# Y products three chunks ahead and a reordered opening in a fused graph-attention and linear kernel

## The reference

```python
def gnn(input1, input2, adj, a1, a2):
    e = input1 @ a1 + (input2 @ a2).T
    e = jnp.where(e > 0, e, 0.2 * e)
    att = jnp.where(adj > 0, e, -9e15)
    att = jax.nn.softmax(att, axis=1)
    att = att * jnp.sum(adj, axis=1, keepdims=True)
    att = 0.1 * att + 0.9 * adj
    return att @ input2
x = x + gnn(layernorm(x), input2, adj, a1, a2)
x = x + layernorm(x) @ weight.T + bias
```

## Time and profile before

| | us |
|---|---|
| median of 3 runs | 385.27 (384.86 to 386.11) |
| profiled execution | 384.49 |
| its span, first to last instruction | 382.7 |

### The profile page before, as it was taken

One profiled execution on the slowest core, in us unless ns is written; L12 is line 12 of the kernel. 1 busy time (PEld: TensorE's weight loads), 2 busy tenths in 40 slices (PEclk: granted clock), 3 DMA queues, 4 the chain that ended last, 5 costly groups with the idle time before them and its releaser, 6 DMA issues.

```text
span 382.7 us, 8770 instructions
## 1 busy us (share of the span) xinstructions
PE 360.1 (94%) x3195; PEld 313.7 (82%) x3195; DVE 311.0 (81%) x791; ACT 246.9 (65%) x630; POOL 136.3 (36%) x257
## 2 busy tenths in 40 slices
PE   1589999999999999999999999999999999999991
PEld 1477888888888888888888888888888888888880
DVE  5999889989978787796968778698887979889633
ACT  4798989787661947658192856839294776777010
POOL 4598041515250706144160705326070613110111
PEclk9999999999999999999999999999999999999997
DMA  7999996666668989799998988996867610010000
GB/s 254 231 214 213 223 184 143 122 141 122 143 16 163 111 125 146 63 210 18 196 77 151 120 82 188 20 221 50 184 89 118 151 29 15 0 16 16 14 15 16
DMA packets 21769, 44.12 MB, mean 115 GB/s; under 512 B 5078, under 2 KB 13020, under 8 KB 21724
## 3 DMA queue, kind: packets, MB, share of 16 engines
q0 software_dynamic: 9216, 33.56, 61.1%
q1 hardware_dynamic: 12508, 9.98, 9.4%
HBM read 74.97 MB, written 2.11 MB: 201 GB/s over the span
## 4 chain that ended last, share of the span: by engine, by line
PE 85%; DVE 6%; ACT 5%; issue 1%; DMA 1%; SPq 0%; POOLq 0%; POOL 0%; DVEq 0%
PE acc_y L660 23%; PE acc_v L660 22%; PE acc_u L660 22%; PE acc_u L651 6%; PE acc_v L651 6%; PE acc_y L651 4%; ACT steep L488 3%; PE small L645 2%; DVE plus L998 2%; DMA plus<-in 1%; PE turned L620 1%; ACT minus L545 1%; ACT weights_v L536 1%; ACT weights_u L530 0%; DVE plus L875 0%
## 5 line engine op out<-in xcount | busy, mean ns | idle before, releaser
L488 ACT ACTIVATE steep<-s_bc,steep_s 128x256 bf16<-128x256 f32 x512 | 209.2, 497 | 80.8 <-DMA s_bc<-s_rows 74.8
L660 PE MATMUL acc_y<-weights_y,adj_all 128*128 128x257 f16 x896 | 103.7, 275 | 2.0 <-DVE lin L896 1.3
L875 DVE TENSOR_TENSOR plus<-adj_all,steep 128x2048 bf16<-128x2048 bf16 x64 | 78.5, 1226 | 27.1 <-ACT steep L488 27.1
L660 PEld LDWEIGHTS acc_y<-weights_y,adj_all 128*128 128x128 bf16 x896 | 87.5, 98 | 15.6 <-DVE lin L896 1.6
L660 PE MATMUL acc_v<-weights_v,minus 128*128 128x258 f16 x832 | 95.2, 273 | 0.0
L660 PE MATMUL acc_u<-weights_u,plus 128*128 128x258 f16 x816 | 93.3, 273 | 0.0
L660 PEld LDWEIGHTS acc_v<-weights_v,minus 128*128 128x128 bf16 x832 | 80.8, 97 | 11.2
L660 PEld LDWEIGHTS acc_u<-weights_u,plus 128*128 128x128 bf16 x816 | 79.1, 97 | 11.1 <-DVE post_st L932 0.2
L878 DVE TENSOR_TENSOR minus<-adj_all,plus 128x2048 bf16<-128x2048 bf16 x64 | 78.4, 1225 | 2.2
L394 POOL TENSOR_SCALAR post_var<-post_mv 128x2 f32<-128x2 f32 x15 | 3.2, 215 | 178.4 <-DVE post_mv L939 178.4
L352 POOL DMA_DIRECT2D adj_all<-adj x64 | 36.2, 584 | 6.6 <-DMA plus<-in 4.6
(11 more groups left out here) (99 smaller groups left out, 301.8 us busy)
## 6 DMA issues: line engine op xcount, KB each, us to landing
adj_all<-adj POOLq DMA_DIRECT2D x64, 512.0 KB, 14.0
x_pre<-x SPq DMA_DIRECT2D x16, 128.0 KB, 10.6
plus<-in SPq DMA_DIRECT2D x4, 512.0 KB, 5.6
x_res<-x SPq DMA_DIRECT2D x16, 128.0 KB, 11.3
out<-late SPq DMA_DIRECT2D x15, 128.0 KB, 4.1
s_bc<-s_rows SPq DMA_DIRECT2D x11, 128.0 KB, 8.5
s_rows<-pre_s SPq DMA_DIRECT2D x11, 1.0 KB
out<-late SPq DMA_DIRECT2D x2, 64.0 KB, 2.3
```

What stands on the lines that cost most here:

```text
L488: ins = nc.scalar.activation(steep[:, h, k, :], s1_bc[b][:, :], ACT.Relu, bias=steep_s2[:, jt:jt + 1], scale=STEEP)
L660: ends[t] = nc.tensor.matmul(acc[t][:, 0:width], left[:, jt, cols(t)], right[:, jt, :, :].rearrange("p a b -> p (a b)")[:, 0:width], start ...
L875: nc.vector.tensor_tensor(plus[b][:, qs, :], adj_b[f][:, qs, :], steep[:, q % 2, :, :], ALU.is_gt).then_inc(plus_ready, 1)
```

## The change

Y runs one chunk further ahead: `y_chunk(c)` gives the chunk whose Y product stands in slot c, c + 3 up to slot 11 (chunk 14), none in slot 12, and chunk 15 in slot 13. The opening has Y(0) to Y(3). `PAIRED` loses slot 12, which gets the order of the tiles one after the other. The values that wait between `linear_part` and the epilogue (`lin2`, `deg`) get three buffers, and `lin` goes: the first step writes into x_res itself. In a slot with a Y product the whole product now comes ahead of `linear(c-1)`.

The opening changes on every engine. POOL loads adj quarter 0 alone ahead of `row_sums`. SP holds back the second x_pre and both x_res until `wy_ready` 1; the later x_res loads move (`load_res`), two of them between the `store_s1` calls. VectorE has `low_y(0)` right behind the first quarter of s2, `low_y(1)` in the pause for the maximum, `value_u(1)` ahead of the first `low_u`, `linear_part(0)` ahead of `low_v(0)`, and masks(1, 0) and `linear_part(2)` at the head of slot 0. ScalarE has the sign test of quarter 1 ahead of `bd`, quarter 2 behind `value_v(2)`, quarter 3 last. TensorE has Y(0) quarter 0 ahead of the maximum's way, 18 matmuls of constants (`warm`) whose result nobody reads, Y(1)'s last quarter behind the first masked quarter, and Y(3) after the last. `a2_bc` moves from `steep` to a part of `minus[0]` so that the second half of `steep` is free early.

```diff
@@ -37,8 +37,9 @@
 GEN = 31
-PAIRED = range(3, CHUNKS - 2)
+PAIRED = [*range(3, CHUNKS - 4), CHUNKS - 3]
 SPREAD = 5
+AHEAD = 3
@@ -255,6 +255,12 @@
+        def y_chunk(c):
+            if c == CHUNKS - 3:
+                return CHUNKS - 1
+            return c + AHEAD if c + AHEAD < CHUNKS - 1 else None
         def ahead(c, k):
@@ -275,6 +281,10 @@
         def _(sp):
+            def load_res(n, b):
+                sp.wait_ge(y_left, 2 * n - 2)
+                sp.dma_start(x_res[b][:, :, :], x[n]).then_inc(xres_landed[b], 16)
             def store_s1(n, b):
@@ -291,25 +301,27 @@
                 sp.dma_start(in2_f[:, q * QJ:(q + 1) * QJ, :], in2[:, q]).then_inc(in2_landed[q], 16)
+            sp.wait_ge(wy_ready, 1)
             sp.dma_start(x_pre[1][:, :, :], x[1]).then_inc(xpre_landed[1], 16)
...
             store_s1(0, 0)
+            load_res(2, 0)
             store_s1(1, 1)
+            load_res(3, 1)
...
                     sp.dma_start(x_pre[1 - b][:, :, :], x[c + 3]).then_inc(xpre_landed[1 - b], 16)
-                if c + 2 < CHUNKS:
-                    sp.wait_ge(y_left, 2 * c + 2)
-                    sp.dma_start(x_res[b][:, :, :], x[c + 2]).then_inc(xres_landed[b], 16)
                 if c == 0:
...
                     sp.dma_start(bias_bc[:, :], bias.partition_broadcast(P)).then_inc(ffn_w_landed, 16)
+                if c + 4 < CHUNKS:
+                    load_res(c + 4, b)
                 if c >= 2:
@@ -424,9 +436,9 @@
             pool.wait_ge(in2_landed[0], 16)
-            load_adj(0, (0, 1))
+            load_adj(0, (0,))
             row_sums(0, 0)
-            load_adj(0, (2, 3))
+            load_adj(0, (1, 2, 3))
             load_adj(1)
@@ -550,19 +562,19 @@
             sign_tests(0, 0, 0)
+            act.wait_ge(s2_signs, 2)
+            sign_tests(0, 1, 0)
             act.wait_ge(bd_arg_ready, 2)
             nc.scalar.activation(bd[:, :, :], bd_arg[:, :, :], ACT.Exp).then_inc(bd_ready, 1)
             act.wait_ge(bd_ready, 1)
             for q in range(QUARTERS):
                 value_v(q)
+                if q == 2:
+                    sign_tests(0, 2, 0)
                 high_u(q)
                 high_v(q)
-                if q:
-                    if q == 1:
-                        act.wait_ge(s2_signs, 2)
-                    sign_tests(0, q, 0)
-                if q == 2:
-                    copy_spread(1, 1)
+            sign_tests(0, 3, 0)
+            copy_spread(1, 1)
             exps(0, 0)
@@ -734,22 +728,44 @@
-            for q in range(QUARTERS):
+            def warm(count):
+                for _ in range(count):
+                    nc.tensor.matmul(acc_v[0][:, 0:P], ident[:, :], ones[:, :], start=True, stop=True)
+            pe.wait_ge(consts_ready, 1)
+            pe.wait_ge(a_landed, 16)
+            nc.tensor.matmul(a_ps, ones[0:1, :], a_row, start=True, stop=True).then_inc(a_spread, 1)
+            warm(12)
+            spread(0, 0)
+            warm(6)
+            pe.wait_ge(wy_ready, 1)
+            y_quarter(0, 0)
+            pe.wait_ge(smax_ready, 1)
+            nc.tensor.transpose(g_ps[0:1, :], s2_max[:, :], ident[:, :]).then_inc(smax_turned, 1)
+            pe.wait_ge(top_ready, 1)
+            nc.tensor.matmul(g_bc_ps, ones[0:1, :], top[0:1, :], start=True, stop=True).then_inc(top_spread, 1)
+            for q in range(1, QUARTERS):
                 pe.wait_ge(wy_ready, q + 1)
                 y_quarter(0, q)
-            for q in range(QUARTERS):
-                y_quarter(1, q)
-            spread(1, 1)
+            y_quarter(1, 0)
+            y_quarter(1, 1)
+            y_quarter(1, 2)
             pe.wait_ge(g_ready, 1)
...
             masked_quarter(0, 0)
+            y_quarter(1, 3)
             masked_quarter(0, 1)
+            spread(1, 1)
             y_quarter(2, 0)
+            y_quarter(2, 1)
             masked_quarter(0, 2)
-            y_quarter(2, 1)
-            masked_quarter(0, 3)
             y_quarter(2, 2)
             y_quarter(2, 3)
+            masked_quarter(0, 3)
+            for q in range(QUARTERS):
+                y_quarter(3, q)
             spread(2, 0)
@@ -782,7 +798,7 @@
                     masked_pair(acc_v, minus[b], w_v, minus_ready, tile_done, c)
-                    y_pair(c + 2, (f + 2) % BUFS)
+                    y_pair(y_chunk(c), y_chunk(c) % BUFS)
                     linear(c - 1)
@@ -794,11 +810,9 @@
                         product(acc_v[t], minus[b], w_v, t, minus_ready, c).then_inc(tile_done, 1)
-                if ahead(c, 2):
-                    y_product(c + 2, 0, (f + 2) % BUFS)
+                if y_chunk(c) is not None:
+                    y_pair(y_chunk(c), y_chunk(c) % BUFS)
                 linear(c - 1)
-                if ahead(c, 2):
-                    y_product(c + 2, 1, (f + 2) % BUFS)
@@ -885,16 +899,16 @@
                 dve.wait_ge(y_done, g + 1)
-                if n >= 2:
-                    dve.wait_ge(tile_left, g - 3)
-                nc.vector.scalar_tensor_tensor(out=lin[t][:, :], in0=acc_y[t][:, 0:D], scalar=y_scale,
+                if n >= AHEAD:
+                    dve.wait_ge(tile_left, g + 1 - 2 * AHEAD)
+                nc.vector.scalar_tensor_tensor(out=x_res[b][:, t, :], in0=acc_y[t][:, 0:D], scalar=y_scale,
                                                in1=x_res[b][:, t, :], op0=ALU.mult,
                                                op1=ALU.add).then_inc(lin_step, 1)
-                nc.vector.tensor_scalar(deg[b][t][:, :], acc_y[t][:, D:WC], GAMMA, None,
+                nc.vector.tensor_scalar(deg[n % AHEAD][t][:, :], acc_y[t][:, D:WC], GAMMA, None,
                                         ALU.mult).then_inc(lin_step, 1)
                 dve.wait_ge(lin_step, 2 * g + 2)
-                nc.vector.scalar_tensor_tensor(out=lin2[b][t][:, :], in0=acc_y[t][:, WC:WC + D], scalar=y_scale,
-                                               in1=lin[t][:, :], op0=ALU.mult,
+                nc.vector.scalar_tensor_tensor(out=lin2[n % AHEAD][t][:, :], in0=acc_y[t][:, WC:WC + D], scalar=y_scale,
+                                               in1=x_res[b][:, t, :], op0=ALU.mult,
                                                op1=ALU.add).then_inc(y_left, 1)
@@ -1042,7 +1057,7 @@
             nc.vector.tensor_scalar(steep_s2[:, QJ:JT], s2[:, QJ:JT], STEEP, None, ALU.mult).then_inc(s2_signs, 1)
-            low_y(0)
+            low_y(1)
             dve.wait_ge(smax_turned, 1)
@@ -1052,20 +1067,20 @@
                                     ALU.subtract, ALU.mult).then_inc(bd_arg_ready, 1)
-            low_y(1)
             low_y(2)
+            low_y(3)
             dve.wait_ge(bd_ready, 1)
             value_u(0)
-            low_y(3)
+            value_u(1)
             for q in range(QUARTERS):
                 low_u(q)
+                if q == 0:
+                    for t in range(TILES):
+                        linear_part(0, t, 0)
                 low_v(q)
-                if q < QUARTERS - 1:
-                    value_u(q + 1)
-                if q == 0:
-                    for t in range(TILES):
-                        linear_part(0, t, 0)
                 masks(0, q, 0, 0)
+                if q < QUARTERS - 2:
+                    value_u(q + 2)
                 if q == 0:
@@ -1074,13 +1089,19 @@
                 b = f % 2
+                if inner(c) and y_chunk(c - 1) is not None:
+                    for t in range(TILES):
+                        linear_part(y_chunk(c - 1), t, y_chunk(c - 1) % 2)
                 if inner(c):
-                    if ahead(c, 1):
-                        for t in range(TILES):
-                            linear_part(c + 1, t, 1 - b)
                     if c >= 2:
...
                     post_end(c - 1, 1 - b)
+                if not inner(c):
+                    dve.wait_ge(u_low, QUARTERS)
+                    dve.wait_ge(v_low, QUARTERS)
+                    masks(1, 0, 1, 1)
+                    for t in range(TILES):
+                        linear_part(2, t, 0)
                 if ahead(c, 2):
@@ -1096,11 +1117,8 @@
                     return
-                if not inner(c):
-                    dve.wait_ge(u_low, QUARTERS)
-                    dve.wait_ge(v_low, QUARTERS)
-                order = [0, "first", "second", 1, 2, 3] if c == 0 else \
+                order = ["first", "second", 1, 2, 3] if c == 0 else \
                     [0, 1, 2, "first", "second", 3] if c in PAIRED else \
```

More of the change, by code:

```diff
@@ L81, in gnn_ffn @@
         a1_bc = sb("a1_bc", [P, D], F32)
[L82 removed]
+        a2_bc = minus[0][:, 0, :].bitcast(F32)
         bias_bc = sb("bias_bc", [P, D], F32)
@@ L670, in product @@
                 return ins
-            pe.wait_ge(consts_ready, 1)
-            pe.wait_ge(a_landed, 16)
-            nc.tensor.matmul(a_ps, ones[0:1, :], a_row, start=True, stop=True).then_inc(a_spread, 1)
-            spread(0, 0)
-            pe.wait_ge(smax_ready, 1)
```

(28 more changed lines are left out.)

14 lines of the change are left out of this document (5 added, 9 removed).

## The result

The changed kernel takes **390.3 us** (median of 4 runs, 389.5 to 390.8), the one before, beside it, 385.3 (384.9 to 386.1): ratio 1.0128, 95% interval 1.0114 to 1.0143. Slower, as forecast, but by twice the 2.45 us of the forecast and outside the range. The profiled execution took 390.49 us (384.49 before), its span is 388.7 (382.7): 6.0 us to find. Ratios leave out the few runs more than 1.5% above the fastest of their kernel, and the profiles of the two runs with POOL held back, on the third chip, are of such executions (401.6 and 394.9 us).

What follows compares the result with a forecast made beforehand. TensorE, busy 94% of the span, was taken as the bound. 384.49 less 1.45 (opening) plus 3.9 (stall ahead of U(13)) gave 386.9; as a median 385.27 + 2.45 = 387.7 us, 8-in-10 range 385.0 to 389.6.

Steps and rivals of the forecast that it cites:

- The sign: Whole kernel: the change makes it slower, 387.7 us against 385.27; chance of slower 0.75.
- the end's mechanism: Slot 12 without a Y product: U(13) must wait for both epilogues of chunk 12, released by VectorE's bn_stats; 3.9 us.
- the stall: Ahead of U(13) in slot 13: TensorE ready at 313.8, starts at 317.7, a new idle time of 3.9 us.
- I keep the seventh block at 28.9: Opening: seventh adj block lands at 28.9 us, Y(1) quarter 2 ends at 30.7, part of a 1.45 us gain.
- moves no byte out of this stretch: Opening: holding back x_pre[1] and x_res leaves the bytes ahead of adj unchanged, so the seventh block stays at 28.9.
- Rival 3: Opening gains nothing, through the late g chain and bd, or masks 3 us late: net +3.8, 389.1 us; chance 0.10.
- rival 1: After the stall ahead of U(13) the clock falls too: 1.8 us more, 389.5 us; chance 0.16.
- ScalarE is not later: its tests start at 298.88: Slot 12: ScalarE's tests and numerator finish before VectorE wants them, third quarter at 308.9, fourth at 312.1.
- the reference start of 63.30: Start of slot 1 that would leave the kernel's end unchanged: 56.21 plus 7.09 for Y(3) now ahead of it.
- The constants at nothing: Opening: the 18 constant matmuls on TensorE were costed at nothing, at worst 1.3 us, and given no gain.
- Rival 2: Opening: adj blocks land 2.4 us sooner, gain 3.9, net 0, 385.3 us; chance 0.16, of it 0.08 faster.
- Its far end: Opening with adj still earlier, until masks(0,3) bounds it: slot 1 at 57.1, gain 6.2, net -2.3, 383.0 us.

Runs made afterwards that it cites:

- the control of the second chip: The changed kernel run again, nothing altered, as measure for the other runs on that chip: 392.2 us, ratio 1.0187 to the kernel before.

## Why the prediction was wrong

The sign held, and so did the end's mechanism in the main. Two terms failed, worth 2.9 of the 3.5 us between the forecast of the span (+2.45) and its 6.0. Either alone, added to the forecast, would have left the time inside the range, at 389.1 or 389.2; together they make 390.6. The rest is 0.28 us of the stall, 0.15 of slot 12's form, left out of the sum, and 0.2 at the very end.

1. *"I keep the seventh block at 28.9"*: it landed at 30.5, Y(1)2 ended at 32.3 and not 30.7, slot 1 started at 63.34 and not 61.85: 1.49 us. Of this 1.20 is the block: Y(1)'s first half was through at 29.35 (25.81 + 3.54) and quarter 2 started at 30.56. The other 0.3 would have stayed, for Y(1) began at 25.81 and not 24.4, behind a fourth block that came at 22.4 instead of 21.5. I argued that holding x back "moves no byte out of this stretch" and took the landings as given; the runs showed that x had moved ahead of most of adj before, and now moved beside it until 25 us, with adj 0.19 MB behind by then. With the loads issued as before, the block came at 29.2 and slot 1 at 62.00. Rival 3 named this outcome (the opening gains nothing) by other causes; g and bd and the masks were in time, as no idle time after 32.3 shows.
2. *The clock*, rival 1, left out of the sum: 1.42 us in the first profile, 1.4 to 2.6 in nine profiles with the stall unfilled. With the stall filled by constant products it was nothing (7.26 us). I argued from the 3.76 us of the earlier trace rows that "a little less may do nothing"; the stall was not less but 4.2. Nor did the fall always come at the very end: in the control of the second chip the granted clock read 0.50 from 324 us on, 1.7 us ahead of U(13). A forecast whose own stall equals one that did halve the clock should have carried it. The Trainium skill (TensorE: Matmul & The Clock Gate, Part 1: The HAM clock gate) says the array drops to half its clock when it has been idle, as these rows have it; that too should have made rival 1 the likeliest case.
3. *The stall*: forecast 3.9, measured 4.18 idle, of which 4.02 is the named wait. Right in size and releaser (bn_stats), but the size is in part luck, for the pacing was wrong: *"ScalarE is not later: its tests start at 298.88"* was the weak step. The tests start when the row lands, and U(13) comes 18.6 us after that, whatever VectorE has to spare. In the first profile the row came only 0.33 later in the slot than before, in others up to 2.9; then linear(11) waits for ScalarE's copy as well (0.2 to 2.2 us) while the wait ahead of U(13) stays near 4 (3.65 to 4.08). I had taken one landing of a DMA for a property of the slot. It costs 0.3 us in the first profile and up to 2.9 in others. Between profiles of the changed kernel three terms move, the row, the clock and the opening, and not together; how much of the medians' 390.3 to 392.2 each makes stays open.
4. Total work, slots 1 to 11 unchanged, the reference start of 63.30, slots 13 to 15 behind the stall: as forecast, within 0.2 us each. The constants at nothing: no run shows otherwise.

Rival 2 (adj a block earlier) is refuted: the first block did land earlier (13.46 for 14.5), but the second no sooner (16.6 for 16.7), and from the third on each later (19.5 for 19.1). Its far end is also mis-added: it takes masks(0,3) at 46.0, where the list above it has 47.2. Nothing came near it, so nothing hangs on this.

## What to carry to other kernels

A product that covers an epilogue can't be taken from one slot without asking what its successor waits for: one list entry decided between a stall of 4 us and none. Where a stall is forecast, price the clock after it in the same line, from a row in which that engine stood idle as long. Where a wait hangs on one DMA landing, look at that landing in several profiles before taking its time for a constant. And before holding loads back "to make room", ask what they will stand beside later, and compare queues by share of time and in the same size of element, not by GB/s alone.

## What the runs showed of the hardware

- The profile counts a converting load at its converted size: 33.56 MB for adj, in each run. With the 16 engines busy, 9 to 11 us show 335 to 346 GB/s where SP's f32 loads of x are served (four profiles) and 178 to 225 where it is nearly all adj (twelve), 212 to 215 in a steady stage of adj alone (15 to 31 us before).
- A store of one 1-row piece and its load back took 10.6 and 7.6 us beside 2 MB of adj (288.12 to 306.34), and the landing moved by 2.9 us between eleven profiles.
- After 3.8 us and more with next to no products TensorE ran at a granted 0.50 for some 3 to 5.5 us (the 64 products then took 8.67 to 9.83 us, nine profiles); 16 f32 products of constants in the gap, two passes each in the trace, kept it at full pace: 7.26 us.
